# Five normalising stages of a graph-network kernel, rewritten around fused two-input VectorE passes

## The reference, cut to what matters

```python
h = jnp.maximum(_layernorm(x, axis=-1), 0.0)
x = x + L0(h)          # inside: x_norm = layer_norm(h, norm_g, norm_b), two attention layers, Wu
h = jnp.maximum(_layernorm(x, axis=-1), 0.0)
x = x + L1(h)          # two graph convolutions
h = jnp.maximum(_layernorm(x, axis=-1), 0.0)
x = x + L2(h)          # inside: relu(layer_norm(h, g1, be1)) + (h0 @ Wr1 + br1),
                       #         layer_norm(h, g2, be2) + (h1 @ Wr2 + br2)
h = jnp.maximum(_layernorm(x, axis=-1), 0.0)
x = x + L3(h)          # three relational convolutions
```

## Time and profile before

| | us |
|---|---|
| three runs | 4063.90, 4069.36, 4070.57 |
| their median | 4069.36 |
| the profiled execution | 4071.57 |
| its span, first to last instruction | 4069.70 |
| stage t0 | 257.6 to 369.6 |
| stage t3 | 975.3 to 1022.1 |
| stage t5 | 1329.7 to 1369.6 |
| stage t6 | 1858.1 to 1941.8 |
| attention g3 | 2057.4 to 2342.5 |
| stage t7 | 2343.5 to 2466.7 |

### The profile page before, as it was taken

The page is one execution under the profiler, slowest core; times in us unless marked ns, Lnnn a source line. Parts: engine busy times, 40 slices in busy tenths (PEclk is TensorE's granted clock), DMA queues, the critical chain, the costliest instruction groups (busy, mean ns, idle before and its releaser), DMA issues. The chain is left out here.

```text
span 4069.7 us, 55709 instructions
## 1 busy us (share of the span) xinstructions
PE 3319.4 (82%) x21922; PEld 3173.3 (78%) x21923; DVE 1869.0 (46%) x3441; ACT 1090.0 (27%) x1910; POOL 512.4 (13%) x682
## 2 busy tenths in 40 slices
PE   7925588676898568993879926999999999999898
PEld 7814578576898467883768805999999999999898
DVE  6757686665232587756565573222122221321111
ACT  2303233232343232231322211222332221322212
POOL 0001000010110252100211001102121211210110
PEclk9956798587899689996889957999999999999999
DMA  1221210022112221111110032223232322321312
GB/s 24 53 63 33 32 38 15 13 65 87 41 44 61 80 45 47 42 31 67 39 31 28 20 118 87 61 71 90 82 94 64 84 57 60 89 59 47 104 54 71
DMA packets 279466, 232.87 MB, mean 57 GB/s; under 512 B 108947, under 2 KB 264508, under 8 KB 279175
## 3 DMA queue, kind: packets, MB, share of 16 engines
q1 hardware_dynamic: 166225, 163.33, 14.7%
q10 hardware_dynamic: 112950, 65.63, 5.8%
HBM read 194.98 MB, written 33.94 MB: 56 GB/s over the span
## 5 line engine op out<-in xcount | busy, mean ns | idle before, releaser
L2414 PE MATMUL psum<-p_w_hi,h_lo 128*125 128x384 f32 (+1 forms) x1680 | 533.7, 318 | 48.2 <-POOL p_w_lo L2183 32.5
L2415 PE MATMUL psum<-p_w_lo,h_hi 128*125 128x384 f32 (+1 forms) x1680 | 531.7, 317 | 0.0
L2417 PE MATMUL psum<-p_w_hi,h_hi 128*125 128x384 f32 (+1 forms) x1680 | 530.7, 316 | 0.0
L2475 PE MATMUL psum<-p_c_st,p_v_lo 125*128 125x312 f32 (+1 forms) x1800 | 510.3, 309 | 13.7 <-ACT p_c_st L2242 13.7
L1808 PE MATMUL psum<-v,g_e 125*125 125x193 f32 (+4 forms) x2320 | 428.7, 344 | 102.2 <-DVE g_e L1613 102.0
L2475 PE MATMUL psum<-p_c_st,p_v_hi 125*128 125x312 f32 (+1 forms) x1800 | 508.6, 308 | 0.0
L1808 PEld LDWEIGHTS psum<-v,g_e 125*125 125x125 f32 x2320 | 387.3, 203 | 135.0 <-DVE g_e L1613 56.1
L2242 ACT CAST p_c_st<-p_c 125x624 fp32r<-125x624 uint16 (+2 forms) x450 | 286.0, 679 | 390.2 <-DMA p_c<-c_dram 208.1
L2324 DVE TENSOR_TENSOR p_v_lo<-psum,p_v_hi 125x384 fp32r<-125x384 f32 (+1 forms) x210 | 109.0, 519 | 549.7 <-ACT p_v_hi L2258 549.7
L2414 PEld LDWEIGHTS psum<-p_w_hi,h_lo 128*125 128x125 f32 x1680 | 316.4, 188 | 53.7 <-POOL p_w_lo L2183 30.0
L2475 PEld LDWEIGHTS psum<-p_c_st,p_v_lo 125*128 125x128 f32 x1800 | 337.5, 190 | 15.8 <-ACT p_c_st L2242 15.8
(11 more groups left out here) (253 smaller groups left out, 6237.1 us busy)
## 6 DMA issues: line engine op xcount, KB each, us to landing
p_c<-c_dram ACTq DMA_DIRECT2D x45, 761.7 KB
p_w_raw<-in_L_gnn_w_rel_dram SPq DMA_DIRECT2D x96, 192.0 KB
p_c<-c_dram ACTq DMA_DIRECT2D x30, 610.4 KB
p_c<-c_dram ACTq DMA_DIRECT2D x15, 766.6 KB
p_w_raw<-in_L_gnn_W_dram SPq DMA_DIRECT2D x84, 128.0 KB
c_dram<-counts SPq DMA_DIRECT2D x15, 610.4 KB
res_dram<-g_fin SPq DMA_DIRECT2D x70, 125.0 KB
p_scale<-inv_dram SPq DMA_DIRECT2D x54, 156.0 KB, 3.2
```

The source lines that it names most:

```text
L2414: pe.matmul(prod, lo[:, b, cols], w_hi[:, slot, :w], start=(b == 0), stop=False)
L2415: pe.matmul(prod, hi[:, b, cols], w_lo[:, slot, :w], start=False, stop=False)
L2417: ins = pe.matmul(prod, hi[:, b, cols], w_hi[:, slot, :w], start=False, stop=end)
L2475: return pe.matmul(ps[:, 2 + u % UB, :n], v[:, b, off:off + size], counts_at[:, :n], start=start, stop=stop, skip_group_check=True)
```

## The change

The five normalising calls go to a new function, `norm_rows`; the other two calls of `turn_rows` stay. Its `kind` says what a stage does: "both" for t0, "plain" for t3 and t5, "gain" for t6, "next" for t7.

- VectorE passes are `scalar_tensor_tensor`, one instruction with two tensor inputs and a column of scalars: `(row - mean) * gain`, then `row * rstd + shift`. In t7 the second of them is `row * rstd + (res + x)`.
- Where there is no gain, the norm and the clip are one ScalarE `Relu` with `scale = rstd` and `bias = -mean * rstd`. In t6 the clip is a ScalarE `Relu` by itself.
- In t6 GpSimd adds `res`; in t7 GpSimd adds `res` and `x` to each other ahead of the rows.
- The second norm of t0 and t7 writes into a ring of three tiles, no more in place.
- No instruction waits for the one just before it with `settle`; each step has its own semaphore, and the steps of several tiles are interleaved.
- In t7 both added tensors have two buffers each, so four loads are ahead of the first use. The shift `be2` is added to `f_bias` in attention g3 (`more`), by one broadcast load and one VectorE addition.

```diff
+def norm_rows(nc, k, tag, width, rows, ht, kind, gain=None, res=None, x=None, x_out=None, ht2=None, low=None, table=None):
+    kb = width // 128
+    halves = 2
+    second = kind in ("both", "next")
+    own = rows.shape[0] != P
+    padded = not own and len(rows.shape) == 4
+    n_st = rows.shape[2] if padded else 2
+    span = width // n_st
+    R = 3
...
+        rs = sb("rows", [P, NT, width]) if own else rows
+        gb = sb("gb", [P, 2, width]) if gain else None
+        add_r = sb("add_r", [P, 2, width]) if res is not None else None
+        add_x = sb("add_x", [P, 2, width]) if x is not None else None
+        ring = sb("ring", [P, R, width]) if second else None
+        st1 = sb("st1", [P, NT, n_st, 6])
+        st2 = sb("st2", [P, NT, 2, 6])
+        mv = sb("mv", [P, 2, NT, 2])
+        rstd = sb("rstd", [P, 2, NT])
+        less = sb("less", [P, 2, NT])
...
+        lag = {"plain": 1, "gain": 2, "next": 3}
+        def turning(i):
+            if kind == "both":
+                return [(o, t) for o, t in ((0, i - 2), (1, i - 3)) if 0 <= t < NT]
+            t = i - lag[kind]
+            return [(0, t)] if 0 <= t < NT else []
+        last = NT + 6
+        order = [ot for i in range(last) for ot in turning(i)]
...
+                for i in range(NT + 2):
+                    t = i - 2
+                    if t >= 0 and x_out is not None:
+                        sp.wait_ge(y_made, t + 1)
+                        sp.dma_start(x_out.rearrange("(t p) f -> p t f", p=P)[:, t], row(t)).then_inc(stored, 16)
+                    if tables and i == 8:
+                        tables.store(sp)
+                    if i < NT and res is not None:
+                        if i >= 2:
+                            sp.wait_ge(y_made, i - 1)
+                        sp.dma_start(add_r[:, i % 2], res.rearrange("(t p) f -> p t f", p=P)[:, i]).then_inc(r_in[i % 2], 16)
+                    if i < NT and x is not None:
+                        sp.dma_start(add_x[:, i % 2], x.rearrange("(t p) f -> p t f", p=P)[:, i]).then_inc(x_in[i % 2], 16)
+                if x_out is not None:
...
+            def _(pool):
+                if kind == "gain":
+                    for t in range(NT):
+                        pool.wait_ge(r_in[t % 2], 16 * (t // 2 + 1))
+                        pool.wait_ge(clipped, t + 1)
+                        pool.tensor_tensor(row(t), row(t), like(add_r[:, t % 2]), ALU.add).then_inc(y_made, 1)
+                if kind == "next":
+                    for t in range(NT):
+                        pool.wait_ge(r_in[t % 2], 16 * (t // 2 + 1))
+                        pool.wait_ge(x_in[t % 2], 16 * (t // 2 + 1))
+                        pool.tensor_tensor(add_r[:, t % 2], add_r[:, t % 2], add_x[:, t % 2], ALU.add).then_inc(both_in, 1)
...
+                def minus1(t):
+                    dve.wait_ge(inv1, t + 1)
+                    dve.scalar_tensor_tensor(less[:, 0, t:t + 1], mv[:, 0, t, 0:1], -1.0, rstd[:, 0, t:t + 1],
+                                             ALU.mult, ALU.mult).then_inc(less1, 1)
+                def scale1(t):
+                    dve.wait_ge(gained, 32)
+                    dve.wait_ge(var1, t + 1)
+                    dve.scalar_tensor_tensor(row(t), row(t), mv[:, 0, t, 0:1], like(gb[:, 0]), ALU.subtract,
+                                             ALU.mult).then_inc(scaled, 1)
+                def shift1(t):
+                    dve.wait_ge(scaled, t + 1)
+                    dve.wait_ge(inv1, t + 1)
+                    if kind == "next":
+                        dve.wait_ge(both_in, t + 1)
+                        dve.scalar_tensor_tensor(row(t), row(t), rstd[:, 0, t:t + 1], add_r[:, t % 2], ALU.mult,
+                                                 ALU.add).then_inc(y_made, 1)
+                    else:
+                        dve.scalar_tensor_tensor(row(t), row(t), rstd[:, 0, t:t + 1], like(gb[:, 1]), ALU.mult,
+                                                 ALU.add).then_inc(shifted, 1)
...
+                def scale2(t):
+                    dve.wait_ge(gained, 32)
+                    dve.wait_ge(var2, t + 1)
+                    if t >= R:
+                        dve.wait_ge(turned, halves * (order.index((1, t - R)) + 1))
+                    dve.scalar_tensor_tensor(ring[:, t % R], row(t), mv[:, 1, t, 0:1], gb[:, 0], ALU.subtract,
+                                             ALU.mult).then_inc(scaled2, 1)
+                def shift2(t):
+                    dve.wait_ge(scaled2, t + 1)
+                    dve.wait_ge(inv2, t + 1)
+                    dve.scalar_tensor_tensor(ring[:, t % R], ring[:, t % R], rstd[:, 1, t:t + 1], gb[:, 1], ALU.mult,
+                                             ALU.add).then_inc(ring_made, 1)
...
+                for i in range(last):
+                    if at(i):
+                        stats1(i)
+                    if at(i - 1):
+                        inverse1(i - 1)
+                    if kind in ("gain", "next") and at(i - 1):
+                        scale1(i - 1)
+                    if at(i):
+                        mean1(i)
+                    if kind in ("plain", "both") and at(i - 1):
+                        minus1(i - 1)
+                    if kind in ("gain", "next") and at(i - 1):
+                        shift1(i - 1)
+                    if second and at(i - 2):
+                        stats2(i - 2)
+                    if second and at(i - 3):
+                        inverse2(i - 3)
+                    if kind == "both" and at(i - 3):
+                        scale2(i - 3)
+                    if second and at(i - 2):
+                        mean2(i - 2)
+                    if kind == "next" and at(i - 3):
+                        minus2(i - 3)
+                    if kind == "both" and at(i - 3):
+                        shift2(i - 3)
+                    if tables and 3 <= i < 7:
+                        tables.combine(dve, (2 * i - 6, 2 * i - 5))
+                    if low is not None:
+                        for _, t in turning(i - 2):
+                            take_low(t)
...
+                    if i < NT:
+                        act.wait_ge(var1, i + 1)
+                        act.activation(rstd[:, 0, i:i + 1], mv[:, 0, i, 1:2], ACT.Sqrt, bias=k.eps[0:P, 0:1]).then_inc(root1, 1)
+                    t = i - 1
+                    if 0 <= t < NT and kind in ("plain", "both"):
+                        act.wait_ge(less1, t + 1)
+                        act.activation(row(t), row(t), ACT.Relu, bias=less[:, 0, t:t + 1],
+                                       scale=rstd[:, 0, t:t + 1]).then_inc(y_made, 1)
+                    if 0 <= t < NT and kind == "gain":
+                        act.wait_ge(shifted, t + 1)
+                        act.activation(row(t), row(t), ACT.Relu).then_inc(clipped, 1)
+                    t = i - 2
+                    if 0 <= t < NT and second:
+                        act.wait_ge(var2, t + 1)
+                        act.activation(rstd[:, 1, t:t + 1], mv[:, 1, t, 1:2], ACT.Sqrt, bias=k.eps[0:P, 0:1]).then_inc(root2, 1)
+                    t = i - 3
+                    if 0 <= t < NT and kind == "next":
+                        act.wait_ge(less2, t + 1)
+                        if t >= R:
+                            act.wait_ge(turned, halves * (order.index((0, t - R)) + 1))
+                        act.activation(ring[:, t % R], row(t), ACT.Relu, bias=less[:, 1, t:t + 1],
+                                       scale=rstd[:, 1, t:t + 1]).then_inc(ring_made, 1)
+                    if tables and 2 <= i < 6:
+                        tables.round_up(act, (2 * i - 4, 2 * i - 3))
+                    for o, t in turning(i - 1):
+                        take(o, t)
+                        n += 1
...
@@ attention @@
-def attention(nc, k, tag, heads, ch, v, parts, rows=None, given=0, bias=None, diag=None, slots=6, e=None, fill=()):
+def attention(nc, k, tag, heads, ch, v, parts, rows=None, given=0, bias=None, diag=None, slots=6, e=None, fill=(), more=None):
...
+            f_more = sb("f_more", [P, more.shape[0]], F32) if more is not None else None
...
                     at += j.w.shape[1]
+                if more is not None:
+                    sp.dma_start(f_more[:], more.partition_broadcast(P)).then_inc(f_bias_in, 16)
                 for n in range(RAWS, kb):
...
-                        dve.wait_ge(f_bias_in, 16 * len(jobs))
+                        dve.wait_ge(f_bias_in, 16 * (len(jobs) + (more is not None)))
+                    if f == 0 and more is not None:
+                        step(dve.tensor_tensor(f_bias[:], f_bias[:], f_more[:], ALU.add))
@@ build @@
-                            turn_rows(nc, k, "t0", D, a["x"], h_t, ln=True, relu=True, ht2=xn_t,
-                                      gain2=(w["L0_norm_g"], w["L0_norm_b"]))
+                            norm_rows(nc, k, "t0", D, a["x"], h_t, "both", ht2=xn_t,
```

(14 more changed lines are left out.)

134 lines of the change are left out of this document (added).

## The result

The changed kernel takes 4014.99 us (median of four runs, 4013.21 to 4026.57), the kernel before 4068.85 (four runs, 4063.90 to 4070.57): a ratio of 0.9876, with a 95% interval from 0.9855 to 0.9896. That is 53.9 us less. Forecast were 4026, so 43 less, with a range down to 4008.

The account below looks back on a forecast made before the run. TensorE is busy for 82% of the span; VectorE or transfers pace the five changed stages. Terms -19.2, -7.8, 0, -8.6, -8.6, +1.5 sum to -42.7 us from 4071.57: 4028.9, by the runs' median 4026.7, stated as 4026; range 4008 to 4041.

Parts of the forecast that it names:

- t0: First normalising stage: VectorE sets the pace, full iteration 4.75 us instead of 6.90, stop at gain stays; gain 19.2 us.
- t3: Normalising stage: loads become the limit instead of VectorE, last tile takes 6.9 us after its load; gain 7.8 us.
- t5: Normalising stage: loads are and stay the limit; gain 0, from 1 to -1.5 us.
- t6: Normalising stage: VectorE's gain pass waits for GpSimd's addition, cycle 6.1 us instead of 7.06; gain 8.6 us.
- t7: Normalising stage: transfers become the limit, three a tile, 9.15 us; gain 8.6 us, 10 at most.
- g3: Attention g3: the extra be2 broadcast load delays the weight blocks and GpSimd's splits; loss 1.5 us, between 0 and 4.
- The forecast's case: Whole kernel: the stage terms hold, with GpSimd holding up VectorE's two-input passes in t6; 4026 us, chance 0.66.
- A: Rival in t6: GpSimd does not hold up VectorE, cycle 4.25 us, stage gains 24; kernel 4011 us, chance 0.13.
- B: Rival in t6: statistics too wait for GpSimd, cycle about 6.8 us, gain 3; kernel 4032 us, chance 0.13.
- C: Rival on ScalarE: square root and Relu cost two table loads a tile, 2.57 us; kernel about 4067 us, chance 0.03.
- The exclusion: In t6, a VectorE two-input pass and a GpSimd instruction do not overlap, the later waits: cycle 6.1 us, not 4.25.
- Semaphores: End of each stage: more semaphores are cleared, priced at nothing, at most 0.3 us a stage.

Follow-up runs that it names:

- the other order: Changed kernel with t6's next gain pass straight after a shift pass on VectorE, statistics behind it: t6 61.7 us instead of 70.4; 4009.9 us, ratio 0.9862.

## Why the prediction was right

The forecast's case is the one that came; A, B and C did not. The number alone would not have said so: 4015 lies nearer to A's 4011 than to 4026 and at the edge of the forecast's own range, 4014 to 4038. The traces decide. The forecast was 11 us too slow because t0 (6.4) and t6 (3.9) both gained more than it put, and it put 1.5 for g3 that is not seen; in t3 it was 1.0 too hopeful. Step by step:

- **t0.** The stop stays, 22.04 us; after it VectorE runs through; ScalarE and TensorE are hidden. These were right. The term was mis-sized, 19.2 for 25.6, beyond the 21 that it gave at best. From the stop to the last pass it is 340.94 - 305.68 = 35.3 us, not 39.8. The step that failed is "a full iteration is 2 x 1.05 + 2 x 1.0 + five small ones, 4.75". It adds up durations of rows (and these come to 4.70, not 4.75), but VectorE begins an independent instruction before the last one's row ends. Putting dependent instructions in a row takes back 0.41 us of the 0.59. Of the other 2 us, 1.5 are in the loads: gain and shift land 48.5 us after the first issue, not 50.0; the cause of that stays open.
- **t3.** Right: load-bound, the last tile takes 6.96 us where 6.9 was put. The missing 1.0 us is in the end of the loads, put at 1006.5: the row still moves 80 GB/s in the slice of 1006 to 1007 and 18 in the next. Splitting the loads shows what sets their pace.
- **t5.** Right: no gain. The 41.8 us of the first trace come from loads of 3.30 us a tile; the later traces last 39.1 to 40.2.
- **t6.** The exclusion was read rightly from the earlier trace rows. "Gain passes that last about 3 us" became 3.18, the cycle of 6.1 became 5.80, and the term 12.5 for 8.6. Mis-sized were the estimate of GpSimd's addition, 2.4, which is 2.17, and the two-input pass of 1.25, which is 1.14 to 1.20 from start to start; 0.7 more came from gain and shift, which land 10.9 us after the stage's start, not 11.6. B would have had statistics wait; they do not, as the other order shows. A is excluded by the passes of 3.18, and by passes of 1.2 to 1.3 where GpSimd is silent.
- **t7.** Right: three transfers of 3.0 us, 8.99 a tile for 9.15, at 123 to 135 GB/s. The term of 8.6 is 6.8 in the changed kernel's own trace and 9.2 in the others, against the one trace of before. The prediction gave a granted clock of 0.50 for these stretches; t7's in the earlier trace rows is 0.54, and nothing hangs on it.
- **g3.** "A later first GpSimd cast, up to 3 us" was wrong in its place: the first is not late; the third is, at 13.32 us after the stage's first GpSimd instruction instead of 12.15. Whether the stage loses 1.5 us by it stays open.
- **Semaphores.** Priced at nothing: from a stage's last instruction to the next stage's first it is 0.80 to 0.91 us before and 0.88 to 0.97 after, under 0.1 more a stage.
- **C.** Three table loads in all, 1.283 us each: square root and `Relu` change over without one.

What the prediction did not ask is why the transfers are as slow as they are. The three stages that it called transfer-bound hang on how 125 rows are shared out over the DMA engines, and the rows showed it already: a flat rate at a share of 0.3.

## What to carry to other kernels

Before work is moved to GpSimd, ask which instruction of VectorE will stand beside it: here statistics ran on and two-input passes waited, and the order on VectorE alone was worth 8.7 us in a stage of 70, more than taking the addition back to VectorE (6.7). A flat transfer rate at a DMA share of 0.3 points at the transfer's shape: cutting transfers of 125 rows in two gave 11, 13 and 30 us in three stages by their traces, as much as the whole rewriting of the passes. Where the first rows of a stage come late, look also at the last transfer of the stage ahead. When a list of instructions is priced for an engine, take distances from start to start, and ask of each pair whether the second needs the first.

## What the runs showed of the hardware

- A VectorE pass that reads two tensors from SBUF and a GpSimd addition do not overlap: 1.22 us becomes 3.18 beside an addition of 2.17, and a pass that begins with the addition, at 2312.22, waits for it too (2.63 for 1.02). The addition waits likewise when the pass came first (3.22 for 2.17). A column of one element per row waits as well (1.34 for 0.10); statistics (1.39 for four) and a subtraction with one input in PSUM (0.99 for two) do not.
- A stage's loads of 125 rows, one transfer each, move 123 to 135 GB/s in most slices at a DMA share of 0.3; cut into 112 and 13 rows they move 255 to 286 in most.
- A store of 19.5 KB in some 5000 packets takes 10 us, at 2 to 10 GB/s, and the next stage's loads move behind it.
- `Sqrt` and `Relu` alternate on ScalarE without a table load: three loads of 1.283 us in all five stages.
- VectorE's independent instructions begin 0.92 us after a pair of statistics of 1.01, a dependent one after 1.05.
